# Weight-quarter sums on VectorE, edge preparation two units later, edge weights in four pieces, edge lists loaded at unit 8

## What is computed

```python
xn = layernorm(x)
out = xn @ root + bias
for r in range(8):                       # mean over the edges of relation r, by target node
    mask = (edge_type == r)
    sums = segment_sum(xn[src] * mask[:, None], dst, 1250)
    mean = sums / maximum(segment_sum(mask, dst, 1250), 1)[:, None]
    out = out + mean @ weight[r]
# then a gate over [u, xn], a linear attention over xn (Wq, Wk, Wv, Wg, Wo),
# a residual, a second layernorm and one step of an LSTM-like cell (W_i, W_o, W_c)
```

## Time and profile before

| | us |
|---|---|
| median of 3 runs (lowest, highest) | 2199.6 (2197.4, 2200.03) |
| the profiled execution, whole | 2188.48 |
| its span, first to last instruction | 2186.7 |
| TensorE busy in the span | 2118.5 (97%) |
| VectorE, ScalarE, GpSimd busy | 1297.6, 538.6, 808.0 |
| mean granted TensorE clock | 0.987 |

### The profile page before, as it was taken

The page is one execution under the profiler, slowest core; times in us unless marked ns, Lnnn a source line. Parts: engine busy times, 40 slices in busy tenths (PEclk is TensorE's granted clock), DMA queues, the critical chain, the costliest instruction groups (busy, mean ns, idle before and its releaser), DMA issues.

```text
span 2186.7 us, 25371 instructions
## 1 busy us (share of the span) xinstructions
PE 2118.5 (97%) x9562; PEld 1708.9 (78%) x9562; DVE 1297.6 (59%) x1705; ACT 538.6 (25%) x749; POOL 808.0 (37%) x663
## 2 busy tenths in 40 slices
PE   7979897989999999999999999999999999999999
PEld 6767675768888888888877778888988887888887
DVE  5555778665666666666656666773354658534233
ACT  4433353501111111100121211012232313321121
POOL 3248134025555556543646445541211353000000
PEclk9999898999999999999999999999999999999999
DMA  7986675778588888883987878974159998604102
GB/s 273 344 282 196 220 248 173 250 206 303 173 288 309 314 295 308 280 288 116 317 281 270 279 260 296 306 229 163 61 172 263 282 294 270 175 23 126 56 34 80
DMA packets 248145, 497.68 MB, mean 228 GB/s; under 512 B 39442, under 2 KB 71873, under 8 KB 248023
## 3 DMA queue, kind: packets, MB, share of 16 engines
q1 hardware_dynamic: 165782, 279.20, 39.1%
q0 software_dynamic: 65248, 191.13, 26.2%
q10 hardware_dynamic: 16992, 25.73, 3.6%
HBM read 403.60 MB, written 133.45 MB: 246 GB/s over the span
## 4 chain that ended last, share of the span: by engine, by line
PE 90%; DVE 4%; DMA 2%; issue 1%; POOL 1%; SPq 1%; ACT 0%; POOLq 0%; ACTq 0%; DVEq 0%
PE acc L1412 71%; PE acc L1383 12%; PE acc L1407 5%; POOL runs L2375 1%; PE acc L1320 1%; DMA Wraw<-in_L_gnn_weight 1%; DVE Wlo L1708 1%; PE misc L1305 1%; DMA sample_d<-samples 1%; DMA made<-y_d 1%; SPq L861 0%; DVE below L1834 0%; PE tp L1267 0%; DMA runs<-code_d,run_row 0%; PE acc L1420 0%
## 5 line engine op out<-in xcount | busy, mean ns | idle before, releaser
L1412 PE MATMUL acc<-Whi,aThi 128*128 128x512 f32 (+1 forms) x2232 | 882.0, 395 | 0.0
L1412 PE MATMUL acc<-Whi,aTlo 128*128 128x512 f32 (+1 forms) x2232 | 879.1, 394 | 0.0
L1412 PE MATMUL acc<-Wlo,aThi 128*128 128x512 f32 (+1 forms) x2232 | 876.5, 393 | 0.0
L2395 POOL DMA_INDIRECT ring<-y_d,edge x390 | 484.1, 1241 | 425.7 <-DVE U L1984 144.1
L1412 PEld LDWEIGHTS acc<-Whi,aTlo 128*128 128x128 f32 (+1 forms) x2232 | 413.7, 185 | 103.5
L1412 PEld LDWEIGHTS acc<-Wlo,aThi 128*128 128x128 f32 (+1 forms) x2232 | 414.4, 186 | 102.4
L1412 PEld LDWEIGHTS acc<-Whi,aThi 128*128 128x128 f32 (+1 forms) x2232 | 413.6, 185 | 102.0 <-DVE made L1756 0.3
L1708 DVE TENSOR_TENSOR Wlo<-Wraw,Whi 128x1024 fp32r<-128x1024 f32 x176 | 224.0, 1275 | 161.1 <-ACT Whi L1438 160.2
L1383 PE MATMUL acc<-Whi,aThi 128*128 128x512 f32 (+2 forms) x560 | 229.4, 410 | 54.1 <-DVE Wlo L1708 33.1
L1984 DVE SCALAR_TENSOR_TENSOR U<-ring,edge,U 128x1024 f32<-128x1024 f32 x180 | 230.3, 1280 | 31.6 <-DMA ring<-y_d,edge 31.3
L1984 DVE SCALAR_TENSOR_TENSOR odd<-ring,edge,odd 128x1024 f32<-128x1024 f32 x170 | 217.7, 1280 | 36.4 <-DMA ring<-y_d,edge 35.9
(11 more groups left out here) (209 smaller groups left out, 1566.5 us busy)
## 6 DMA issues: line engine op xcount, KB each, us to landing
Wraw<-in_L_gnn_weight SPq DMA_DIRECT2D x80, 512.0 KB, 8.0
y_d<-res SPq DMA_DIRECT2D x80, 256.0 KB, 2.3
Whraw<-in_L_gnn_weight SPq DMA_DIRECT2D x24, 512.0 KB, 6.8
y_d<-made ACTq DMA_DIRECT2D x32, 256.0 KB
Wraw<-in_L_gnn_w_gate SPq DMA_DIRECT2D x16, 512.0 KB, 7.9
y_d<-made ACTq DMA_DIRECT2D x32, 252.0 KB
ring<-y_d,edge POOLq DMA_INDIRECT x390, 6.3
aTraw<-ax_d SPq DMA_DIRECT2D x4, 1250.0 KB, 9.7
```

Source lines behind the costliest of these rows:

```text
L1412: mm = nc.tensor.matmul(to, a[:, k, rows(i)], b[:, s % 2, k, :], start=start, stop=stop)
L2395: pool.indirect_dma_start(ring[:, j % RING, :], None, a, bass.IndirectOffsetOnAxis(ap=index, axis=0), bounds_check=top - 1, oob_is_err=Fal ...
```

## The change

1. `add_quarters` goes from GpSimd to VectorE, the same 32 additions. They stand at units 3 to 5 of the stage before a BE stage (ticks 1 and 5) and at units -1 and 0 for a GA stage, where they were at units 2 to 5 on GpSimd.
2. `edge_at` starts 16 ticks, that is two units, later in both its ranges, and `READS_AT` goes from 43 to 45. With it go SP's stores and loads for the edges (30 to 32, 31 to 33, 62 to 64, 64 to 66) and ScalarE's rank signs. `SENDS_AT` stays.
3. `tables_weights` is cut in four pieces with two hand-made ticks between them: in units the first half's `tables` stands at unit 97 tick 3, the pieces at 97.7, 98.2, 98.6 and 99.2; `lo_w` of granule 41 is at 98.4. Before: `tables` at 95.3, `tables_weights` whole at 97.0. Second half: `tables` 126.0, pieces 126.3, 126.7, 127.3, 127.7; before 124.0 and 125.5.
4. At the start, SP loads the fifth granule before x1 and all eight before x2, and the edge lists at unit 8. GpSimd does the sums of rows 1 and 2 before the edge codes.

```diff
-SUM_BESIDE = {BE_: (2, 2, 3, 3, 4, 5), GA_: (-1, 0)}
+SUM_BESIDE = {BE_: ((3, 1), (3, 5), (4, 1), (4, 5), (5, 1), (5, 5)), GA_: ((-1, 5), (0, 5))}
...
-READS_AT = 43
+READS_AT = 45
...
     if q < 36:
-        return divmod(212 + (8 * (q - 17) + k) * 21 // 16, 8)
-    return divmod(424 + (8 * (q - 36) + k) * 61 // 32, 8)
+        return divmod(228 + (8 * (q - 17) + k) * 21 // 16, 8)
+    return divmod(440 + (8 * (q - 36) + k) * 61 // 32, 8)
...
             load_x(0)
-            for n in SPLIT_ORDER[0:4]:
+            for n in SPLIT_ORDER[0:5]:
                 load_w(n)
             load_x(1)
-            load_w(SPLIT_ORDER[4])
-            load_w(SPLIT_ORDER[5])
+            for n in SPLIT_ORDER[5:8]:
+                load_w(n)
             load_x(2)
-            load_w(SPLIT_ORDER[6])
-            load_w(SPLIT_ORDER[7])
             load_x(3)
...
+                if q == 8:
+                    load_raw_edges()
...
+            def add_quarters(s, g, n):
+
+                def add(to, of):
+                    nc.vector.tensor_tensor(to, to, of, ALU.add).then_inc(w_sum, 1)
+
+                kind, at = STAGE[s][0], GRAN * s + g
+                if kind == BE_ and n > 1:
+                    dve.wait_ge(w_sum, sums_to(s, g, n - 1))
+                    add(granule(Wraw, at) if n == 2 else granule(Whraw, at + 2), granule(Wraw, at + 2 if n == 2 else at))
+                    return
+                dve.wait_ge(w_raw[at % (2 * GRAN)], raw_to(at, 2))
+                if kind == BE_:
+                    dve.wait_ge(w_raw[(at + 2) % (2 * GRAN)], raw_to(at + 2, 2))
+                    add(granule(Wraw, at + 2), granule(Whraw, at))
+                else:
+                    add(granule(Wraw, at), granule(Whraw, at))
...
+                    if (q, k) in SUMS_AT:
+                        add_quarters(*SUMS_AT[q, k])
...
-                        if (q, k) == edge_at(59 + 15 * h, 1):
-                            tables_weights(h)
+                        for piece in range(4):
+                            if (q, k) == edge_at(58 + 15 * h, 4 + 2 * piece):
+                                tables_weights(h, piece)
...
+            for t in (1, 2):
+                rows_sum(t)
             edge_codes()
...
             for q in range(BLOCK_UNITS):
-                for s, g, n in SUMS_AT.get(q, ()):
-                    add_quarters(s, g, n)
```

More of the change, by code:

```diff
@@ L1917, in tables, with tables_weights @@
                 chain(nc.vector.tensor_scalar(weigh[:, :, :], top, 0.0, None, ALU.is_ge))
-            def tables_weights(h):
+            def tables_weights(h, step_of):
                 top = top_codes[:, h, :, :]
                 rows_of = table[:, h, :, 0:2 * WIDE].rearrange("p t (c e) -> p t c e", e=2)
[L1923 to L1927, removed]
-                    step.inc(nc.vector.tensor_reduce(inv[:, r, :], of_r[:, r, :, :], AX.X, ALU.add))
-                step.wait(dve)
-                chain(nc.vector.tensor_scalar(inv[:, :, :], inv[:, :, :], 1.0, None, ALU.max))
-                chain(nc.vector.reciprocal(inv[:, :, :], inv[:, :, :]))
-                for r in range(HALF_R):
-                    step.inc(nc.vector.tensor_tensor(of_r[:, r, :, :], of_r[:, r, :, :],
-                                                     inv[:, r, :].unsqueeze(2).to_broadcast([128, T, WIDE]), ALU.mult))
-                step.wait(dve)
-                for r in (0, 2):
-                    step.inc(nc.vector.tensor_tensor(of_r[:, r, :, :], of_r[:, r, :, :], of_r[:, r + 1, :, :], ALU.add))
-                step.wait(dve)
-                step.inc(nc.vector.tensor_tensor(rows_of[:, :, :, 1].bitcast(F32), of_r[:, 0, :, :], of_r[:, 2, :, :],
-                                                 ALU.add))
-                step.inc(nc.vector.tensor_copy(table[:, h, :, 2 * WIDE], nodes[:, :]))
-                step.inc(nc.vector.tensor_copy(table[:, h, :, 2 * WIDE + 1].bitcast(F32), cnt[:, h, :]))
-                step.wait(dve)
-                dve.sem_inc(tabled, 1)
@@ new lines, in tables_weights @@
+                if step_of == 0:
+                    for r in range(HALF_R):
+                        step.inc(nc.vector.scalar_tensor_tensor(of_r[:, r, :, :], relation[:, :, :], float(r),
+                                                                weigh[:, :, :], ALU.is_equal, ALU.mult))
+                    step.wait(dve)
+                elif step_of == 1:
+                    for r in range(HALF_R):
+                        step.inc(nc.vector.tensor_reduce(inv[:, r, :], of_r[:, r, :, :], AX.X, ALU.add))
+                    step.wait(dve)
+                    chain(nc.vector.tensor_scalar(inv[:, :, :], inv[:, :, :], 1.0, None, ALU.max))
+                    chain(nc.vector.reciprocal(inv[:, :, :], inv[:, :, :]))
+                elif step_of == 2:
+                    for r in range(HALF_R):
+                        step.inc(nc.vector.tensor_tensor(of_r[:, r, :, :], of_r[:, r, :, :],
+                                                         inv[:, r, :].unsqueeze(2).to_broadcast([128, T, WIDE]),
+                                                         ALU.mult))
+                    step.wait(dve)
+                else:
+                    for r in (0, 2):
+                        step.inc(nc.vector.tensor_tensor(of_r[:, r, :, :], of_r[:, r, :, :], of_r[:, r + 1, :, :],
+                                                         ALU.add))
+                    step.wait(dve)
+                    step.inc(nc.vector.tensor_tensor(rows_of[:, :, :, 1].bitcast(F32), of_r[:, 0, :, :],
+                                                     of_r[:, 2, :, :], ALU.add))
+                    step.inc(nc.vector.tensor_copy(table[:, h, :, 2 * WIDE], nodes[:, :]))
+                    step.inc(nc.vector.tensor_copy(table[:, h, :, 2 * WIDE + 1].bitcast(F32), cnt[:, h, :]))
+                    step.wait(dve)
+                    dve.sem_inc(tabled, 1)
```

34 lines of the change are left out of this document (10 added, 24 removed).

## The result

The changed kernel takes 2178.84 us in the median of four runs (2173.14 to 2181.09); the kernel before, beside it, 2199.43 (2197.40 to 2200.03). The ratio is 0.9904, 95% interval 0.9884 to 0.9924: 21 us faster by the medians. The forecast was 2178.0 us, within 2168 to 2188. The profiled execution took 2178.85 us, its span 2177.1.

A forecast was written before the change was run, and what follows sets the result against it. The prediction took TensorE, busy 2118.5 of 2186.7 us, to bound the kernel, its weight waits lying almost all before 453 us. Terms of 2.5, 4.0, 4.5, 10 and 0.6 sum to 21.6 us: 2199.6 becomes 2178.0 us, range 2168 to 2188.

The forecast's parts named there:

- start: First units: reordered loads and earlier row sums shorten TensorE's early waits; 2.5 us gained, bounds 0 and 4.
- units 40, 41: Unit 40 is seeded sooner and the wait at its k = 2 goes; 4.0 us gained, bounds 1 and 9.
- units 60, 61: After the reads land, VectorE has less work before granule 25 is done; 4.5 us gained, bounds 1 and 8.
- units 100 to 105: Waits and low clock there fall from 17.7 to 7.5 us; 10 us gained, bounds 5 and 14.
- units 130 to 132: One 6.42 us wait for an eviction becomes two, moved rather than removed; 0.6 us gained, bounds -4 and +4.
- so 1.8 us: Unit 2's wait for ScalarE's eviction shrinks, with one 512 KB load no longer ahead; 1.8 us, bounds 0 and 3.0.
- the 0.7 for x4: Rows 1 and 2 summed before the edge codes bring x4 sooner, removing the 0.75 us wait at 53.80; 0.7 us.
- rival A: Units 2, 40 and 60 start on landings that don't move, so the early gain is swallowed; 2187 us, chance 0.17.
- 0.4 for each addition: Before unit 60, six VectorE additions beside GpSimd's reads lengthen the reads by 0.4 us each, 2.4 in all.
- D: Rival: sums could be hidden as before and tables wait for ScalarE's ranks; time as before, 2199 us, chance 0.04.
- Rival B: VectorE is freed more than counted, so the waits at 100 and 130 halve; 2168 us, chance 0.12.
- C: Rival: VectorE stands at a stage's first sum until the quarter lands, delaying later work; 2204 us and more, chance 0.05.

The follow-up runs named there:

- e0_after: The changed kernel run once more, unchanged, for a second profile: 2175.68 us, ratio 0.9914 to the kernel before.
- e1_old_start: The changed kernel with its start as before (old load order, edge codes ahead of the sums of rows 1 and 2): 2176.51 us, ratio 0.9911.
- e2_codes_last: The changed kernel with the edge codes behind all the row sums on GpSimd, new loads kept: 2174.27 us, ratio 0.9900.
- e3_sums_only: The kernel before with only the sums of weight quarters moved to VectorE, at the changed kernel's ticks: 2180.46 us, ratio 0.9916.
- e8_both_apart: The changed kernel with each BE stage's second granule split one unit sooner and `tables_weights` pieces moved later in both halves: 2169.86 us, ratio 0.9872.
- e8_again: The kernel of e8_both_apart run once more, unchanged: 2164.71 us, ratio 0.9864.
- e7_split7: The changed kernel with the second granule of each BE stage split one unit sooner (offset 7 instead of 8): 2173.50 us, ratio 0.9894.
- e4_rest_only: The changed kernel with the sums back on GpSimd at their old units, the rest of the change kept: 2192.27 us, ratio 0.9977.

## Why the prediction was right, and where not

The total was hit to 1 us, with luck in it. The terms were not all hit: two were too small, three too large, and they cancel. The second measurement, e0_after, has a gain of 19 us. Here each stands beside the stages of the table (before: the mean of two traces; after: of after, e0_after, e1_old_start and e2_codes_last).

```
term                predicted   measured
start                  2.5         0      (2.0 at unit 17, lost by unit 36)
units 40, 41           4.0         3.6    (36 to 42)
units 60, 61           4.5         7.7    (42 to 99)
units 100 to 105      10          11.0    (99 to 129)
units 130 to 132       0.6        -0.9    (129 to 139)
sum                   21.6        21.5
```

That the two sums agree is chance too: the 0 of the start stands for a difference that drowns in the spread, and the times give 19 to 21.

*The start.* The step "so 1.8 us" and the 0.7 for x4 were right where they were read: the four traces with the old start reach unit 17 at 71.8 us in the mean, the ten with the new one at 69.8, and unit 2 waits 2.07 us in after instead of 3.99. They reach unit 36 at 141.6 and 141.9. The spread there is 13 us in the first group and 5 in the second, so a gain of 2 us can't be seen there, and none is; by the medians e1_old_start is 0.8 us slower than e0_after, within the noise. The forecast wrote "a start made early can be lost in their backlog" and yet took the term whole; rival A had this half right. The 5.92 us at 78.25 in after, at unit 18, may be one of the places where it goes: all nine traces with the new loads and the edge codes between the sums of rows 2 and 3 wait there, 3.7 to 6.1 us, and none of the other five by more than 0.2. e2_codes_last, one of these five, waits 6.01 us at unit 20 instead (after: 3.69) and reaches unit 36 at 143.2, within the spread.

*Units 40 and 41.* 3.6 for 4.0. Unit 40's wait is there, 4.77 us in after and 5.2 to 7.0 in the other three, with none at its k = 2, as forecast. From the start of unit 36 to that of unit 40 the four traces take 18.9 us in the mean, 2.4 less than the two of before, where 2.3 were forecast. But it is not explained: the sums alone gave 0 here, and so did the rest alone (30.6 and 29.8), and with the sums shortened it was 28.9. In e3_sums_only VectorE stood 2.6 and 1.0 us for quarters to land. With two traces of the same kernel 2.2 us apart (26.1 and 28.3 in e8_both_apart and e8_again), this term is left as fitting by number only.

*Units 60 and 61.* This is the step that was mis-sized most, by 3.2 us, and in two places. From the first read to the first work on the landed rows the forecast had 37.9 us; it was 216.66 - 181.23 = 35.4. It had added 2.4 for six additions beside the reads, at 0.4 each. Timeline of GpSimd in after, reads with sums of VectorE beside them from 201.88 on:

```profile
181.23 3.43 POOL L2386 DMA_INDIRECT runs<-code_d,run_row  x1 [79.94 <-DVEq L1863]
184.96 1.71 POOL L2386 DMA_INDIRECT runs<-code_d,run_row  x1 [0.30 <-issue]
...
206.92 1.00 POOL L2386 DMA_INDIRECT runs<-code_d,run_row  x1 [0.30 <-issue]
208.22 1.20 POOL L2386 DMA_INDIRECT runs<-code_d,run_row  x1 [0.30 <-issue]
```

The additions cost the reads 0.2 us here, all together. The Trainium skill (SBUF — State Buffer, Who interferes with whom) had said they would cost nothing, and that the term would be 2.4 larger by that. The size came out near it, but the traces don't agree with the reason: a sum does hold a read back. Timelines of e7_split7, a read and the sum beside it, and of after, the sum beside the read at 208.22:

```profile
195.76 1.56 POOL L2386 DMA_INDIRECT runs<-code_d,run_row  x1 [0.30 <-issue]
```

```profile
195.23 1.23 DVE L1751 TENSOR_TENSOR Wraw<-Wraw,Whraw 128x1024 f32<-128x1024 f32 x1 [6.00 <-DMA Whraw<-in_L_gnn_weight]
```

```profile
207.32 1.23 DVE L1751 TENSOR_TENSOR Wraw<-Wraw,Whraw 128x1024 f32<-128x1024 f32 x1 [1.70 <-DMA Whraw<-in_L_gnn_weight]
```

The read at 195.76 starts when the sum has 0.70 us left and takes 0.56 more than 1.00; the one at 208.22 starts with 0.33 left and takes 0.20 more; that of the earlier trace rows starts with 2.70 us of a spread left and takes 2.57 more. In all 14 traces a read that starts beside a sum, a low part or a spread takes the rest of that operation less 0.13 us on top of its 1.00, to within 0.03 us (the first of the 20 reads 0.3 more), and one that has started before the operation takes 1.00. So the forecast rightly set the row of 3.57 us against the rule, but 0.4 for each addition was the wrong price: once a read has been held to the end of one sum, the next reads, 1.3 us apart, start with under 0.15 us left of sums that are 1.26 apart. The five sums beside the reads cost 0.2 us in after and 1.1 in e7_split7.

The other place is plain arithmetic: what VectorE does from the landing to the end of granule 25 was written as 17.0 us "at most", but the terms listed there (1.5, 1.25, two of 3.95, three of 0.6, two of 1.22) add to 14.9, and the trace has 231.43 - 216.66 = 14.8. Against these two stands the first read, which came 5.3 us later behind unit 36 than before (mean of the four traces against the two), where 4.2 were forecast.

*Units 100 to 105.* The best step. The predicted remainder was 7.5 us; units 99 to 106 took 26.6 us, 7.1 over 7 x 2.79. Before, they took 37.6, 18.0 over, where the forecast had 17.7. One wait of 4.15 us instead of 4.7 stands at the predicted place with the predicted neighbour in VectorE's order; the second, 1.3 us at 105, is not in after (0.75 us in e0_after, and there for ScalarE). The sums' engine carries a part, and so do the pieces apart with the later preparation: 5.9 us alone, 7.5 alone.

*Units 130 to 132.* The two waits came, at 131 and 132, as forecast, with 2.91 and 2.62 us in place of 1.7 and 3.8. They cost 0.9 us more than the one before, since the low clock is paid behind each: without its waits the stage takes 31.4 us in after and 29.4 in before, where ten undisturbed units take 27.9.

*The rivals.* D falls by e3_sums_only and e4_rest_only. Rival B is not seen: the waits at 100 and at 131 and 132 are not half of what was counted (4.15 for 4.7; 5.5 together for 5.5). And `top_of` could not shrink: its steps take 0.3 us beside a sum of GpSimd as well. Timeline of VectorE in before, a step beside the sum at 323.14:

```profile
323.81 0.30 DVE L1896 MAX8 top_codes<-held 128x8 f32<-128x128 f32 x1
```

So "while it adds, VectorE stands still" holds for some of its operations only: `count_below` (0.86 us) and the evictions (0.69) keep their length too. C's mechanism exists in small (VectorE stands 5.61 us for a quarter before a first sum at 201.88 in after), and no wait of TensorE follows it before 225.27. Its price was summed wrongly: 5.4 us beyond the 8.35 are 13.8 us after the release, not 12.

*The own time of the profiled execution.* The forecast put the gain on the median, not on the profiled 2188.48 us, and that was what kept it right. The execution profiled before was 10.4 us ahead at unit 139 of the second trace (478.9 and 489.3), 9.8 of them up to unit 36. None of this touches the stages where the sum was made.

## What to carry to other kernels

When an engine's work moves, price it twice: what it takes there, and what its absence gives to the engine it shared something with; here 32 additions took 39 us of VectorE, and its busy time rose only from 1297.6 to 1307.1, since its other work took 30 less. When a wait is an instruction standing behind others in one engine's order, move those others to where that engine stands idle itself, and then look for the next wait before counting the gain: the split moved alone (e7_split7) gave its 4 us back to a bank that ScalarE seeded late, the first half's pieces moved (e8_both_apart) gave 6 of 8 us back at the next stage; all of them moved gave 14 us between units 42 and 139. And trace the same kernel twice before explaining a stretch that is full of transfers.

## What the runs showed of the hardware that was not expected

- A step of `tables` or a low part that starts beside an addition of GpSimd takes its own time and the rest of that addition: 0.37 becomes 2.47 with 2.24 left (before), 1.22 becomes 3.00 with 1.9 left, and 1.49 becomes 6.48 where three additions follow without a gap (e4_rest_only). `top_of`, `count_below`, the reductions of `run_half` and the evictions are not held.
- GpSimd's reads are held in the same way by VectorE's sums, low parts and spreads: 1.00 us and the rest of the operation less 0.13, whether that writes the fp32r type (low parts, spreads) or f32 (sums). Beside sums that follow each other only the first read held pays much.
- The stretch of units 17 to 36, with the DMA engines busy at 0.93 to 0.99, moved much the same, 25.3 and 26.0 MB, in 77 and in 87 us in two executions of the same kernel.
